# A new order in the routing half of a convolution and mixture-of-experts block, with the image added to its convolution by an accumulating DMA

## The reference, cut to what matters

```python
x = x + conv(_ln_c(x))          # depthwise 3x3, weights made per image; conv adds its own input too
t = tokens(x)                   # 32768 tokens of 128
t = t + moe(_ln_t(t))           # 8 experts, 128 -> 512 -> 128, exact gelu, the best 2 by softmax
x = images(t)
```

## Time and profile before

| | us |
|---|---|
| median of 3 runs | 1751.96 (1745.91 to 1754.96) |
| the profiled execution | 1765.64 |
| its span | 1763.9 |
| routing half, with the table behind it | 0 to 716 |
| expert half | 716 to 1664.4 |
| last part | 1664.4 to 1763.9 |

### The profile page before, as it was taken

The page is one execution under the profiler, slowest core; times in us unless marked ns, Lnnn a source line. Parts: engine busy times, 40 slices in busy tenths (PEclk is TensorE's granted clock), DMA queues, the critical chain, the costliest instruction groups (busy, mean ns, idle before and its releaser), DMA issues.

```text
span 1763.9 us, 45712 instructions
## 1 busy us (share of the span) xinstructions
PE 1534.5 (87%) x12190; PEld 1137.3 (64%) x12191; DVE 1373.4 (78%) x2855; ACT 1059.2 (60%) x2331; POOL 993.0 (56%) x1061
## 2 busy tenths in 40 slices
PE   4799888888798836899999999999999999999655
PEld 2344444544454421788888888888888888888644
DVE  1578878678778873788888888888889888888634
ACT  3577656556557520677777777777777777776300
POOL 1004545334455464577777777777777777777400
PEclk9899889889889855899999999999999999999866
DMA  3201211111121013211111111111111111110299
GB/s 123 72 26 59 64 59 61 50 60 49 52 68 59 30 40 119 64 41 43 42 44 46 41 38 43 38 44 42 41 44 41 45 41 44 46 40 8 71 360 332
DMA packets 90599, 115.79 MB, mean 66 GB/s; under 512 B 15278, under 2 KB 71754, under 8 KB 90551
## 3 DMA queue, kind: packets, MB, share of 16 engines
q1 hardware_dynamic: 65752, 62.29, 12.6%
q0 software_dynamic: 18176, 34.27, 6.1%
q10 hardware_dynamic: 6624, 18.69, 2.7%
HBM read 60.22 MB, written 58.61 MB: 67 GB/s over the span
## 4 chain that ended last, share of the span: by engine, by line
POOL 33%; issue 23%; PE 17%; DVE 11%; ACT 7%; DMA 4%; POOLq 1%; SPq 1%; another core or an unknown queue 1%; DVEq 0%; ACTq 0%
POOL xn L462 13%; POOL token_out L474 12%; POOL yt L469 8%; PE psV L752 6%; PE psV L710 4%; DMA ye<-token_out 4%; DVE x L1014 3%; PE psT L737 3%; PE psG L739 2%; ACT spent L560 2%; PE psA L701 1%; ACT lnv L528 1%; ACT sd L532 1%; ACT sq L537 1%
## 5 line engine op out<-in xcount | busy, mean ns | idle before, releaser
L1210 DVE TENSOR_TENSOR gl<-g,gh 128x512 f16<-128x512 f32 x624 | 477.9, 805 | 107.2 <-ACT gh L646 101.8
L450 POOL DMA_INDIRECT rows_by_pair<-rows,idx x256 | 273.8, 1070 | 407.0 <-issue 274.2
L474 POOL DMA_INDIRECT token_out<-yt,rt x312 | 340.3, 1091 | 186.5 <-POOL yt L469 132.7
L646 ACT ACTIVATE gh<-g 128x512 f16<-128x512 f32 x468 | 276.1, 624 | 17.2
L752 PE MATMUL psV<-lp,diag 128*128 128x512 f32 x512 | 260.4, 639 | 23.3 <-ACT cv L553 12.6
L639 ACT ACTIVATE g<-psV 128x512 f32<-128x512 f32 x312 | 184.9, 597 | 139.2 <-PE psV L858 121.8
L462 POOL TENSOR_SCALAR xn<-rt 128x128 f32<-128x128 f32 x312 | 240.3, 776 | 27.1 <-DMA rt<-rows_by_pair 23.6
L639 ACT ACTIVATE g<-psT 128x512 f32<-128x512 f32 x312 | 183.3, 597 | 110.7 <-DVE gl L1210 67.2
L879 PE MATMUL psR<-wall,gh 128*128 x1248 | 223.9, 274 | 18.5 <-issue 9.9
L879 PE MATMUL psG<-wall,gh 128*128 x1248 | 223.0, 273 | 0.0
L880 PE MATMUL psG<-wall,gl 128*128 x1248 | 214.3, 219 | 0.0
(11 more groups left out here) (220 smaller groups left out, 3063.9 us busy)
## 6 DMA issues: line engine op xcount, KB each, us to landing
rt<-rows_by_pair SPq DMA_DIRECT2D x156, 133.0 KB, 2.1
xb<-in_x_dram SPq DMA_DIRECT2D x32, 512.0 KB, 3.3
ye<-token_out SPq DMA_DIRECT2D x32, 512.0 KB, 9.9
out_dram<-oe ACTq DMA_DIRECT2D x32, 512.0 KB, 6.1
token_out<-yt,rt POOLq DMA_INDIRECT x312
rows_by_pair<-rows,idx POOLq DMA_INDIRECT x256
stage<-in_L_ffn_W_dram SPq DMA_DIRECT2D x1, 2048.0 KB, 8.2
rows_by_pair<-pad_rows SPq DMA_DIRECT2D x15, 133.0 KB
```

Of the source, the lines that this page charges most:

```text
L450: gp.indirect_dma_start(rows_dram, bass.IndirectOffsetOnAxis(ap=idx[p][:, b:b + 1].bitcast(U32), axis=0), rows[p][:, b, :], None).then_inc ...
L474: gp.indirect_dma_start(y_dram, bass.IndirectOffsetOnAxis(ap=rt[r][:, b, ID:ID + 1].bitcast(U32), axis=0), yt[r][:, b, :], None, bounds_ch ...
L646: sc_.activation(gh[side][q][:, cols], g[side][:, cols], ACT.Copy).then_inc(hi_act, 1)
L1210: v.tensor_tensor(gl[side][q][:, cols], g[side][:, cols], gh[side][q][:, cols], ALU.subtract).then_inc(lo_done, 1)
```

## The change

- **The image is added by a DMA.** ScalarE's `take` writes the convolution straight to `x1`. GpSimd then issues `dma_start` with `accum_op=ADD`, which reads the image from DRAM once more and adds it to `x1` in SBUF. VectorE's `window` waits for that DMA (`x_added`) and not for its own `add_image`; `cv` and `x_used` are gone, and SyncE reloads `xb` when `centre` has read it.
- **GpSimd's order.** The 16 scatters of a unit are cut into groups of 5, 9 and 2; the image additions stand between them: nine scatters of the older unit, addition 0, two scatters, then the wait for `routed_ready` of the newer unit with its first five scatters, then addition 1. One step more is run at the end.
- **VectorE's order** is new (below). `means` goes to ScalarE (`token_means`), `shifts` is done once for both images, and the two weights of a token come from two exponentials of ScalarE: ten short instructions go from `weigh`, `means`, `shifts` and `number` and three come in. `weigh` is now the last of a step.
- **ScalarE's and TensorE's orders** are new. `tap_logits` is done in one piece.
- **Places in `y_dram`.** A token's place is now (its partition) * 8 + (its block), so that partition p of `ye` takes one piece of 4096 bytes.

```diff
@@ SyncE @@
-                    sp.wait_ge(x_used, 4 * t + j + 1)
+                    sp.wait_ge(xc_ready, 4 * t + j + 1)
                     load(4 * t + j + 4, j)
...
-                sp.dma_start(ye[j][:, :, :], y_dram.rearrange("(n b p) d -> n p b d", ...
+                sp.dma_start(ye[j][:, :, :], y_dram.rearrange("(n p b) d -> n p b d", ...
@@ GpSimd @@
-            with pool.Fori(0, NU // 2, 1) as t:
-                for p in range(2):
-                    pool.wait_ge(routed_ready, routed)
-                    pool.wait_ge(kept, images)
-                    for b in range(NB2):
-                        gp.indirect_dma_start(rows_dram, ...
+            def add_image(st_, k):
+                j = 2 * st_.slot(2) + k
+                pool.wait_ge(cv_ready, st_.count(2, 4, 2 * k + 2))
+                pool.sem_inc(conv_seen, 1)
+                n = st_.count(2, 2, k)
+                gp.dma_start(x1[j][:, :], x_v[n] if st_.fixed else x_v[bass.ds(n, 1)].rearrange("a c m -> (a c) m"), accum_op=ALU.add).then_inc(x_added[j], 16)
+            def scatter(st_, stage, first, end):
+                p = st_.slot(stage)
+                if first == 0:
+                    pool.wait_ge(routed_ready, st_.count(stage, 1, 1))
+                    pool.sem_inc(routed_seen, 1)
+                for b in range(first, end):
+                    gp.indirect_dma_start(rows_dram, ...
+            def step(st_):
+                if st_.on(5):
+                    scatter(st_, 5, 5, 14)
+                if st_.on(2):
+                    add_image(st_, 0)
+                if st_.on(5):
+                    scatter(st_, 5, 14, NB2)
+                if st_.on(4):
+                    scatter(st_, 4, 0, 5)
+                if st_.on(2):
+                    add_image(st_, 1)
+            run_steps(pool, step, 1)
@@ ScalarE @@
-                    act.wait_ge(x_used, st_.count(2, 2, k - 1))
-                sc_.activation(cv[k][:, h * HALF:(h + 1) * HALF], psConv, ...
+                    act.wait_ge(tok_ready, st_.count(2, 2, k - 3))
+                sc_.activation(x1[2 * st_.slot(2) + k][:, h * HALF:(h + 1) * HALF], psConv, ...
@@ TensorE, step @@
+                    if k == 1 and st_.on(1):
+                        centre(st_, 1)
                     if st_.on(3):
                         turn(st_, k)
...
+                if st_.on(1):
+                    tap_logits(st_)
+                if st_.next().on(1):
+                    centre(st_.next(), 0)
+                if st_.on(2):
+                    conv(st_, 1, 1, N_PE - 1, N_PE)
@@ VectorE @@
-            def add_image(st_, k):
-                dve.wait_ge(cv_ready, st_.count(2, 4, 2 * k + 2))
-                v.tensor_tensor(x1[j][:, :], cv[k][:, :], xb[j][:, :], ALU.add).then_inc(x_used, 1)
...
-                    dve.wait_ge(x_used, n + 1)
+                    dve.wait_ge(x_added[j], 16 * (st_.turns(stage) + 1))
@@ VectorE, the new step @@
+                if st_.on(3):
+                    window(st_, 3, 1, 0, N_DVE)
+                if st_.on(4):
+                    first_choice(st_)
                 if st_.on(1):
                     norm(st_, 0)
+                if st_.on(4):
+                    second_choice(st_)
                 if st_.on(2):
+                    window(st_, 2, 0, 0, N_DVE - 1)
                 if st_.on(1):
                     norm(st_, 1)
                 if st_.on(4):
                     place(st_)
                 if st_.on(1):
                     split_pooled(st_)
                 if st_.on(4):
+                    number(st_)
+                if st_.on(1):
+                    tap_differences(st_)
                 if st_.on(3):
+                    shifts(st_)
                 if st_.on(1):
                     tap_softmax(st_)
                 if st_.on(2):
+                    window(st_, 2, 0, N_DVE - 1, N_DVE)
+                if st_.on(4):
+                    weigh(st_)
```

More of the change, by code:

```diff
@@ L294, in slot, with run_steps @@
                 return (self.r - (stage - 1)) % 2
-        def run_steps(eng, step):
+        def run_steps(eng, step, more=0):
             for s in range(FIRST):
@@ L301, in run_steps @@
                     step(Step(t, r))
-            for s in range(LAST, NU + 3):
+            for s in range(LAST, NU + 3 + more):
                 step(Step(s // 2, s % 2))
@@ L579, in step @@
                     diagonals(st_, 0)
[L580 to L602, removed]
@@ L692, in _, with centre @@
             pe.wait_ge(s_setup_dve, 2)
-            def centre(st_, k, h):
+            def centre(st_, k):
                 j = 2 * st_.slot(1) + k
[L697 to L703, removed]
+                pe.wait_ge(x_in[j], 16 * (st_.turns(1) + 1))
+                if not st_.fixed or st_.t + st_.r + k > 0:
+                    pe.wait_ge(l_ready, st_.count(1, 2, k))
+                for h in range(2):
+                    last = te.matmul(psA[:, h * HALF:(h + 1) * HALF], centre_w[:, :], xb[j][:, h * HALF:(h + 1) * HALF], start=True, stop=True)
+                last.then_inc(xc_ready, 1)
             def variance(st_, k, h):
@@ L740, in turn, with conv @@
                 last.then_inc(tok_ready, 1)
[L742 removed]
+            def conv(st_, k, h, first, end):
                 j = 2 * st_.slot(2) + k
[L745 removed]
+                if first == 0:
                     if h == 0:
@@ L749, in conv @@
                         pe.wait_ge(cv_ready, st_.count(2, 4, 2 * k + h))
[L750 to L754, removed]
+                for m in range(first, end):
+                    dy, dx = divmod(PE_TAPS[m], 3)
+                    y = dy + h * HH // 2
+                    ins = te.matmul(psConv.rearrange("p (h w) -> p h w", w=WW), diag[k][:, m, :], lp[j][:, y:y + HH // 2, dx:dx + WW],
+                                    start=(m == 0), stop=(m == N_PE - 1))
+                if end == N_PE:
                     ins.then_inc(conv_ready, 1)
@@ L775, in step @@
                 if st_.first:
-                    for h in range(2):
-                        centre(st_, 0, h)
+                    centre(st_, 0)
                 for k in range(2):
+                    if k == 1 and st_.on(1):
+                        centre(st_, 1)
                     if st_.on(3):
@@ L998, in tap_softmax, with window @@
                 c_tap.end()
[L1000 to L1006 removed]
+            def window(st_, stage, k, first, end):
                 j, n = 2 * st_.slot(stage) + k, st_.count(stage, 2, k)
[L1009 removed]
+                if first == 0:
                     c_win.begin(n)
[L1011 to L1012 removed]
+                    dve.wait_ge(x_added[j], 16 * (st_.turns(stage) + 1))
+                for m in range(first, end):
                     dy, dx = divmod(DVE_TAPS[m], 3)
```

243 lines of the change are left out of this document (129 added, 114 removed).

## The result

The changed kernel takes 1863.26 us (median; 1859.06 to 1870.08), the kernel before beside it 1748.93 (1745.84 to 1754.96): 6.55% slower, ratio 1.0655 [1.062, 1.069]. The profiled execution took 1863.87 us, its span 1862.2. The forecast was 1819 (1768 to 1865): the sign is right and the time inside the range, but near its end. Between the two profiled spans the change costs 98.3 us, where the sum said 67; between the medians it costs 114. The profiled execution of the kernel before was 16.7 us above its median here, the one of the changed kernel 0.6. In the trace of experiment 1, whose routing half is that of the kernel before, the twelve steps of the earlier trace rows take 438.4 us and not 446.1, so that some of the difference is that one execution.

The account below looks back on a forecast made before the run. A routing-half step chained through VectorE and TensorE, and full DMA engines in the last part, were taken to bound the kernel. 1765.6 + 82 - 15 = 1832.6 us; the median, 13.7 lower, 1819 (1768 to 1865).

Parts of the forecast that it names:

- VectorE's list: Routing half, VectorE's work in one step without waits: 30.9 us before, 27.4 us after the change.
- The pause: VectorE stands each step from weigh's end until five scatters and addition 1 are through: 14.6 us (11.2 to 17.4).
- Issue and landing: Addition 1 on GpSimd in each step: issue 1.3 us, landing 4.8 us (2.9 to 7).
- the copy price: Landing of addition 1 priced as a plain copy: 3.9 us, against 5.6 us with twice the data time.
- The waits behind the pause: VectorE's waits between norm 0 and norm 1 and for the exponential: 1 us a step (0 to 4).
- The start of the half: Routing half up to the first weigh, where additions cost no scatters: +5 us (-5 to +12).
- The last part: Behind the expert half, with DMA engines full: loads of ye get cheaper per MB, -15 us (-10 to -21).
- The rival in which it gains nothing: Last part: something other than piece size limits it, so -15 falls away, total 1834 us; chance 0.2.
- Short ring: Routing half: the order costs little, step 38.5 to 40.5 us, total about 1770; chance 0.14.
- Long chain: Norm 0 to norm 1 binds too, or addition 0 is late: step 46 to 49 us, about 1882; chance 0.12.
- Faster: The last part pays for a routing half with step below about 37 us, total 1722; chance of faster 0.10.
- one ring: Routing half, closed once a step: VectorE's list, five scatters, one addition; step 43.0 us against 37.2.

Follow-up runs that it names:

- experiment 1: The kernel before with only the places in y_dram changed: 1740.15 us, ratio 0.9921.
- experiment 3: The changed kernel with VectorE adding the image in place ahead of the taps, no adding DMA: 1781.37 us, ratio 1.0151.
- 6: The changed kernel with scatters in groups of 1, 9 and 6, so one scatter stands ahead of addition 1: 1795.23 us, ratio 1.0216.
- experiment 10: The changed kernel with the adding DMA replaced by a plain copy, without accumulate: 1840.5 us, ratio 1.0474.
- experiment 2: The kernel before, all its orders kept, with the image added by accumulating DMA: 1819.64 us, ratio 1.0369.
- experiment 4: The changed kernel with VectorE adding the image, no adding DMA, and weigh right behind number: 1733.23 us, ratio 0.9901.
- experiments 8 and 9: The changed kernel with addition 1 ahead of the routed_ready wait, scatters cut eight and eight: 1791.16 us; the same with weigh right behind number: 1778.6 us.
- experiment 7: The changed kernel with addition 1 issued ahead of the routed_ready wait and the five scatters: 1813.23 us, ratio 1.0342.

## Why the prediction was right, and where its sizes were off

The mechanism is the one that was forecast: VectorE stands between weigh and the first tap until five scatters and an addition are through. The total fell inside the range with some luck, for the sizes were off in both directions and the 41 us that the order costs by itself (experiment 3) were not in the sum.

**VectorE's list.** The waits of VectorE in the twelve steps, first of the changed kernel (161.31 to 698.26), then of the kernel before (139.67 to 585.76):

```profile
DVE x L1058 <- DMA x<-in_x_dram: 151.6, 12, 13.6
DVE lp L1016 <- ACT sd L552: 42.2, 12, 6.0
```

```profile
DVE lp L969 <- ACT sd L532: 47.4, 23, 4.5
```

With the short ones the waits of the changed kernel are 208.9 us, 17.4 a step. Forecast 27.4 us a step for the list, measured 44.75 - 17.4 = 27.3. Right.

**The pause.** Forecast 14.6, in the row 12.9, mean wait 12.6. The five scatters were priced too high: 7.5 from one slow row, 6.06 measured. The page of the kernel before has 1.07 us as the mean of a scatter, so that five are 6.9 there; while VectorE stands they run at the best pace that the earlier trace rows show, 0.97 + 0.30. Issue and landing were forecast at 1.3 + 4.8 = 6.1, measured 5.88 (0.98 and 4.9). That scatters and addition are this wait is shown by 6 and 10: fewer scatters ahead, or a cheaper DMA, and the step is shorter by 4.9 of 5.1 and by 1.3. The landing came out right on a misread row: the prediction took a scatter to land 2.4 after its busy time, but the 0.30 of the earlier trace rows lies before the last scatter and the 2.08 runs from its start (1662.27), so that it landed 1.1 after it was issued (at 1663.24). By the prediction's own way of adding, the copy price would have been 2.6 and not 3.9, and 4.3 with twice the data time. Measured are 3.7 for the copy and 4.7 for the addition. The Trainium skill (Collectives: The Full Stack, part 3) gives "two source reads" as the reason why an add in a collective is slow; the trace agrees in the doubled time of the engines, and no run here shows where the second read queues.

**The waits behind the pause.** Forecast 1.0 (0 to 4), measured 17.4 - 12.6 = 4.8, above its bounds; 42.2 / 12 = 3.5 of it is norm 1 waiting for the deviation. Of the terms of a step this one was sized worst: 3.8 too low, some 46 us in twelve steps. The forecast took all waits out of the list and put 1 us back, though VectorE already waited 47.4 us for the deviation in these steps of the kernel before, 4.0 a step; the change hardly altered that. What its own mechanism (TensorE is idle and its clock falls) adds was not worked out. `centre` alone takes 3.75 at 1.2 GHz and 1.88 at 2.4 (the row of experiment 2), and 1.9 is most of the 2.46 that norm 1 waits in the step shown; turn, variance and half a convolution follow in the same chain. Over the stretch 0.83 was granted, against 0.89. No run changes the clock alone, so its share is an estimate. The pause was forecast 1.7 too high and by luck hid half of the error: step 43.0 forecast, 44.75 measured, +21 us in twelve steps.

**The start of the half.** Forecast +5 (-5 to +12), measured +21.6, outside its bounds. In experiment 3 (the order, no DMA) the first weigh ends at 141.56, +1.9; in 2 (the DMA, the old order) at 154.88, +15.2. So most of it is the addition's. VectorE waits for additions four times before the first weigh, 29.1 us in all (10.2, 8.7, 4.0 and 6.1), where the forecast had some 6 against a shorter list; with the plain copy of experiment 10 the first weigh ends at 150.10. The step without stage 1: forecast +6, measured +4.3.

**The last part.** Forecast -15 (-10 to -21), measured -14.2, and -14 alone in 1. The reason is the one given: the price per MB of ye fell, to that of the stores. At that price the prediction's sum would have taken 21 us off; the last part gained 14, and the engines are less full than before (DMA share 0.98, not 1.07), so that the middle value of -15 was partly luck. The rival in which it gains nothing is refuted: the traffic holds 416 to 424 GB/s where it was 337 on average. The Trainium skill (DMA: Bandwidth & Descriptors, where 436 GB/s comes from) has about 358 GB/s as the bound of such transfers; the trace contradicts it for one core alone on the chip, and lies just under that page's fabric figure of 436.

**The other rivals.** *Short ring*: its step of 38.5 to 40.5 needs scatters at the best pace and a landing of 2.9; the first came true, the second not (4.7). *Long chain*: its step of 46 to 49 was not reached in the mean, but single steps took 46.5 to 47.6, with turn 1 wholly at half speed (0.45 us a product and not 0.31, from 322 to 326 us). *Faster* needed the scatters to be issued while VectorE works; with weigh early and without the DMA (experiment 4) that gave 1733.

**What the prediction did not see.** It took the new order as harmless but for the pause. Experiment 3 shows 41 us from the order alone (1781.37 against 1740.15), and experiment 2 shows 69 from the DMA in the old order: -14, +41 and +69 make +96 of the measured +114, so that some 18 us come only from the two together. The prediction's one ring gave nearly the same step, but it is not the only one in this kernel: `keep` waits for the first eight scatters as well, in the changed kernel 43.3 us from 200 to 650, hidden there behind the pause: in the step shown ScalarE then waits another 7.2 us for norm 0.

## What to carry to other kernels

Taking an operation off a busy engine gains nothing if the engine must then wait for it: VectorE lost 54 us of work and gained 205.8 us of waiting for DMAs. Before a DMA takes the place of an instruction, count what lies in front of it in its queue and follow the queue round until it closes; the step can't be shorter than that ring, though other waits can make it longer (experiments 8 and 9). Where a chain leaves TensorE idle, price what comes behind the pause at both clock levels. And time a layout edit like the places in `y_dram` by itself: it was a gain that the rest of the change hid.

## What the runs showed that was not expected

- **Waits that pass late behind a row of scatters.** In experiments 3 and 4 ScalarE stood in front of the means of image 1 until 1.1 to 2.6 us after the last of the 16 scatters had left GpSimd, though TensorE's records have that turn finished some us before. In experiment 2 VectorE (up to 5.7 us) and ScalarE (up to 7.0) mostly stood until 1.2 to 1.8 us after it. The work that is waited for seems not to be what is late, for it happens without any: where VectorE works on the table behind the routing half, each of its short instructions waits only for the one before, on VectorE itself. In the kernel before, VectorE, then GpSimd's last scatter of the half:

```profile
663.18 0.18 DVE L1160 TENSOR_REDUCE tst<-sel 128x1 f32<-128x28 f32 x1
...
673.72 0.16 DVE L1166 TENSOR_TENSOR tt<-tt,grows_down 128x2 f32<-128x2 f32 x1 [1.23 <-DVE grows_down L1165]
675.12 0.19 DVE L1167 SCALAR_TENSOR_TENSOR trow<-tt,trow 128x2 f32<-128x2 f32 x1 [1.24 <-issue]
...
693.76 0.16 DVE L1175 SCALAR_TENSOR_TENSOR tb<-tt,tb 128x2 f32<-128x2 f32 x1
...
687.82 0.96 POOL L450 DMA_INDIRECT rows_by_pair<-rows,idx  x1 [0.30 <-issue]
```

  From 663.4 to 692.7 us these instructions follow each other mostly every 1.4 us, before and after it every 0.2, while GpSimd sends scatters without a break until 688.8. In experiment 3 the same happens inside a step: L1099, which waits for the VectorE instruction before it and nothing else, stood 3.87 us until 244.24, 1.1 after the last scatter. It doesn't follow every such row of scatters: in the step of the changed kernel shown above the choices behind norm 0 run without it. Experiment 4 shows that earlier scatters shorten the step; by what path a row of scatters delays a wait was not found.
- **The traffic of the last part**: with pieces of 4096 bytes on both sides one core moves 418 to 424 GB/s, reads and writes together, in the middle of the part, and 394 on average; with 512 bytes on one side 337 on average.
- **Landing under scatters**: the median of an addition is 5.5 us, but 6.7 in experiment 7, where scatters run beside and ahead of it; addition 0 in the rows there took 433.10 - 425.12 = 8.0.
- **What limits experiments 8 and 9** (39.3 and 38.4 a step) was not taken apart. Several short waits share it.
